# A static order of five engines laid out anew, with points of their own for each stream and for the first pair

## What is computed

```python
def reference(x, ...):
    # tok: byte embedding and six hashed n-gram embeddings, then a dense encoder
    for i, n in enumerate((3, 4, 5, 6, 7, 8)):
        idx = ngram_hash(x, n, 25000)            # float32 weighted sum mod vocab
        acc[:, :s - n + 1] += ngram_emb[i][idx] / n * sigmoid(gates[i])
    h = concat([byte_emb[x], acc / 6]) @ W_enc + b_enc
    # tower: three layers of retention (4 heads of 32, decay folded into rotary q and k) and a gelu ffn
    X = layernorm(h)
    for l in range(3):
        Y = msr(layernorm(X) * ln1_w + ln1_b, ...) + X
        X = gelu(layernorm(Y) * ln2_w + ln2_b @ ffn_w1 + ffn_b1) @ ffn_w2 + ffn_b2 + Y
    h = h + X
    # experts: each token goes to the one of 8 experts with the largest logit
    e = argmax(layernorm(h) @ Wg + bg)
    return h + relu(layernorm(h) @ W1[e] + b1[e]) @ W2[e] + b2[e]
```

## Time and profile before

| | |
|---|---|
| median of 3 runs | 2562.33 us (2554.43, 2562.33, 2565.30) |
| span of the profiled execution | 2420.6 us, 52515 instructions |
| own time of the profiled execution | not given by the page; the median lies 141.7 us above its span |
| TensorE matmul | 2230.0 us (92%) |
| VectorE | 1880.2 us (78%) |
| GpSimd | 1763.7 us (73%) |
| ScalarE | 1551.0 us (64%) |
| the chain that ended last | TensorE 74%, GpSimd 9%, VectorE 7%, issue 5% |
| TensorE's granted clock, mean | 0.979 of full |

### The profile page before, as it was taken

One profiled execution on the slowest core, in us unless ns is written; L12 is line 12 of the kernel. 1 busy time (PEld: TensorE's weight loads), 2 busy tenths in 40 slices (PEclk: granted clock), 3 DMA queues, 4 the chain that ended last, 5 costly groups with the idle time before them and its releaser, 6 DMA issues.

```text
span 2420.6 us, 52515 instructions
## 1 busy us (share of the span) xinstructions
PE 2230.0 (92%) x18308; PEld 1947.2 (80%) x18308; DVE 1880.2 (78%) x5639; ACT 1551.0 (64%) x4990; POOL 1763.7 (73%) x1764
## 2 busy tenths in 40 slices
PE   1579999999999999999999999999999999997984
PEld 0368888888888888888888888888888888886874
DVE  5757788888787888888888888787888888766543
ACT  0256677776767677777777767767677777763442
POOL 5687677777777777778777777777777774333777
PEclk9799999999999999999999999999999999997997
DMA  3552031313122222212131313121221111002875
GB/s 116 193 176 69 24 112 28 112 29 112 27 74 66 72 69 71 70 54 89 27 113 28 112 27 112 29 91 48 72 68 36 33 28 36 1 30 79 256 228 158
DMA packets 110817, 192.19 MB, mean 79 GB/s; under 512 B 24421, under 2 KB 45287, under 8 KB 110449
## 3 DMA queue, kind: packets, MB, share of 16 engines
q1 hardware_dynamic: 66928, 97.96, 11.7%
q0 software_dynamic: 33280, 67.45, 10.0%
q10 hardware_dynamic: 10368, 23.67, 3.2%
HBM read 100.30 MB, written 89.73 MB: 79 GB/s over the span
## 4 chain that ended last, share of the span: by engine, by line
PE 74%; POOL 9%; DVE 7%; issue 5%; ACT 3%; DMA 2%; ACTq 1%; POOLq 0%; SPq 0%; DVEq 0%
PE psum L1294 64%; PE psum L1315 7%; POOL grams L669 3%; PE psum L1368 3%; POOL gr L704 3%; POOL out L731 2%; DVE hid L1141 2%; ACT qm L790 1%; ACT qkT L788 1%; DMA out<-h,e_id 1%; ACT xn L801 1%; DVE side_n L1092 1%; DVE qk L1120 0%; POOL rstd L680 0%; DVE hid L1117 0%
## 5 line engine op out<-in xcount | busy, mean ns | idle before, releaser
L669 POOL DMA_INDIRECT grams<-gram_table,idx_all x768 | 779.1, 1014 | 187.7 <-issue 183.0
L1294 PE MATMUL psum<-xT,lw 128*128 128x256 f32 x1920 | 481.2, 384 | 0.1
L704 POOL TENSOR_TENSOR gr<-ms,con 128x8 f32<-128x8 f32 x192 | 319.2, 1663 | 133.1 <-DVE ms L1146 128.4
L1294 PE MATMUL psum<-lw,hid 128*128 128x129 f32 x3072 | 390.7, 276 | 3.4 <-ACT hid L820 3.4
L1294 PEld LDWEIGHTS psum<-lw,hid 128*128 128x128 f32 x3072 | 370.7, 192 | 12.9 <-issue 5.6
L680 POOL TENSOR_TENSOR rstd<-ss,con 128x2 f32<-128x2 f32 x320 | 233.5, 732 | 195.0 <-ACT squares L764 192.7
L1294 PEld LDWEIGHTS psum<-xT,lw 128*128 128x128 f32 x1920 | 340.5, 192 | 32.3 <-ACT xT L776 0.2
L820 ACT ACTIVATE hid<-psum,par 128x256 f32<-128x256 f32 x768 | 307.7, 487 | 43.2 <-PE psum L1294 40.5
L1294 PE MATMUL psum<-lw,xT 128*128 128x256 f32 (+1 forms) x1536 | 288.6, 331 | 6.5 <-ACT xT L776 6.5
L776 ACT ACTIVATE xT<-psum,par 128x256 f32<-128x256 f32 x384 | 213.9, 561 | 121.6 <-PE psum L1315 120.6
L1294 PEld LDWEIGHTS psum<-lw,xT 128*128 128x128 f32 x1536 | 250.5, 192 | 33.3 <-ACT xT L776 7.2
(11 more groups left out here) (223 smaller groups left out, 4721.2 us busy)
## 6 DMA issues: line engine op xcount, KB each, us to landing
routed_rows<-pad SPq DMA_DIRECT2D x265, 264.0 KB
grams<-expert_w ACTq DMA_DIRECT2D x45, 321.0 KB
grams<-gram_table,idx_all POOLq DMA_INDIRECT x768
grams<-routed_rows SPq DMA_DIRECT2D x80, 132.0 KB
qm<-expert_w ACTq DMA_DIRECT2D x27, 321.0 KB
xb<-x SPq DMA_DIRECT2D x32, 256.0 KB, 3.5
lw<-layer_w SPq DMA_DIRECT2D x1, 2503.5 KB, 11.8
routed_rows<-row,slot POOLq DMA_INDIRECT x128, 2.4
```

What stands on the lines that cost most here:

```text
L669: pool.indirect_dma_start(grams[s][:, g, c, :], None, gram_table, bass.IndirectOffsetOnAxis(ap=idx_all[:, g, at:at + 1], axis=0))\
L704: pool.tensor_tensor(gr[s][:, c], ms[s][:, c], const("half")[:, 0:n], ALU.pow).then_inc(y_r[s], 1)
L1294: return pe.matmul(dst, lhsT, rhs, start=start, stop=stop)
```

## The change

The program of each engine keeps its steps, its semaphores and its data; only the points change, and so the order of the steps. The table `AT` has now an entry for each of the four streams (`2 * s + h`) where it had one for each half. The first pair has a table of its own, `FIRST_AT`. The gathers of the first and second pair have a point each (`FIRST_GATHERS`, `NEXT_GATHERS`), and so have the setup steps (`SETUP_AT`). `LAGS`, `EARLY` and `CLOSING` stay. All entries of `AT` have new values; a few rows of the tables stand for all:

```diff
-LATER_GATHERS = (7.05, 12.5, 21.34, 22.17, 59.24, 65.47, 86.1, 94.55, 101.98, 104.91, 113.22, 119.36)
+LATER_GATHERS = (12.54, 16.39, 21.44, 25.43, 65.16, 67.77, 87.75, 97.67, 102.66, 105.89, 115.69, 118.65)
+SETUP_AT = {
+    "pool sums": (29.81, 32.41, -61.5, -39.17),
+    "pool rest": (43.31, 31.31),
+    "dve front": (-19.14, -58.79, -17.76, -68.98, -30.37, -90.72, -58.67, 14.16, 1.3, 22.9, 16.72),
+    "dve middle": (41.91,),
+    "dve back": (47.24, -1.87, -19.85),
+    "dve layer1": (50.64, 37.25),
+    "dve layer2": (68.28, -8.55),
+}
+FIRST_GATHERS = (
+    (-66.45, -47.46, -10.8, -68.66, -29.74, -5.51, 1.84, -28.34, -9.51, -80.01, -15.08, -63.27),
+    (-68.21, -13.83, -32.71, -15.08, -80.07, -14.35, -88.26, -32.05, -43.75, -128.7, -141.88, -3.47),
...
+NEXT_GATHERS = (
+    (27.83, -6.29, -28.85, 25.87, 37.09, -94.35, 42.14, 47.52, -1.13, 50.35, -22.49, 42.25),
...
 AT = {
-    "pe qkT": ((9.86, 8.84, 8.47), (9.32, 11.03, 9.14)),
-    "pe w1": ((5.16, 6.35, 4.1), (5.09, 6.4, 5.9)),
+    "pe qkT": ((11.26, 9.4, 9.79), (8.36, 8.33, 9.76),
+        (8.6, 9.43, 7.91), (10.56, 11.52, 9.22)),
+    "pe w1": ((4.48, 7.83, 5.35), (5.37, 3.46, 6.61),
+        (4.44, 7.87, 6.12), (4.13, 3.57, 7.24)),
...
+FIRST_AT = {
+    "dve xn1": ((10.49, -0.85, -41.79), (-4.3, 5.85, 6.58),
+        (0.74, -59.19, -0.67), (-5.43, -15.7, 3.21)),
+    "dve kv": ((-48.75, -20.26, 12.44), (14.48, 16.61, 10.66),
+        (10.58, 10.83, 0.47), (2.76, 13.62, -19.03)),
+    "dve onehot": ((-14.52,), (18.71,),
+        (33.71,), (-2.47,)),
...
-        def spaced(part, start, step):
+        def spaced(part, name):
             for n, _ in enumerate(part):
-                yield start + step * n
+                yield SETUP_AT[name][n]
...
-        def at(name, h, l=0):
-            return AT[name][h][l]
+        def at(name, it, s, h, l=0):
+            if it == 0:
+                return FIRST_AT[name][2 * s + h][l]
+            return AT[name][2 * s + h][l]
...
-                yield from spaced(mod_sum(hashes[1], REST_MOD), 31.5, 1.5)
-                yield from spaced(mod_rest(hashes[1], REST_QUOT), 39, 1)
+                yield from spaced(mod_sum(hashes[1], REST_MOD), "pool sums")
+                yield from spaced(mod_rest(hashes[1], REST_QUOT), "pool rest")
...
-                    yield (1.25 * n - 15, 30 + 2.6 * n, LATER_GATHERS[n])[min(it, 2)]
+                    yield (FIRST_GATHERS[2 * s + h], NEXT_GATHERS[2 * s + h], LATER_GATHERS)[min(it, 2)][n]
...
-                yield from spaced(hash_front(hashes[1]), 4, 3)
-                yield from spaced(hash_middle(hashes[1], 3), 38, 1)
-                yield from spaced(hash_back(hashes[1], 4), 40, 1)
-                yield from spaced(centred_layer(1), 46, 4)
-                yield from spaced(centred_layer(2), 60, 4)
+                yield from spaced(hash_front(hashes[1]), "dve front")
+                yield from spaced(hash_middle(hashes[1], 3), "dve middle")
+                yield from spaced(hash_back(hashes[1], 4), "dve back")
+                yield from spaced(centred_layer(1), "dve layer1")
+                yield from spaced(centred_layer(2), "dve layer2")
```

More of the change, by code:

```diff
@@ L1105, in attend @@
                 a, b = bank_a(s, h), bank_b(s, h)
-                yield at("dve xn1", h, l)
+                yield at("dve xn1", it, s, h, l)
                 if l == 0:
@@ L1168, in route @@
                 moments = row[s][:, :, H + 1:H + 3]
-                yield at("dve row", h)
+                yield at("dve row", it, s, h)
                 if it:
```

360 lines of the change are left out of this document (280 added, 80 removed), and 35 rows, old and new, of tables (AT, FIRST_GATHERS, NEXT_GATHERS).

## The result

| | us, median (lowest to highest) | runs |
|---|---|---|
| before | 2562.95 (2554.43 to 2565.3) | 4 |
| after | 2611.82 (2603.71 to 2612.71) | 4 |

The ratio is 1.0197 [1.0172, 1.0221]. Forecast were 2549 us and a range of 2532 to 2574.

A forecast was written before the change was run, and what follows sets the result against it. TensorE was taken to bound the kernel from about 200 us, waiting earlier while the four streams fill. Terms -8 - 1.3 - 3 - 0.5 = -12.8 us on 2562.3 gave 2549 us, range 2532 to 2574.

The forecast's parts named there:

- The base: Whole kernel: the 141.7 us between profiled span 2420.6 and median 2562.3 were taken as unchanged time around the span.
- the -8 of the first pair: First pair of batches: -8 us together, bounds -13 to +10, from gathers of pair 1 and the clock.
- The repeating order: Some 14 later pairs: -0.2 us each, -3 us in all, as the wait at scores b2 moves to qkT b2.
- third rival: Repeating pairs: w1 c1 behind qkT b2 starts 1.4 us later each pair, giving 2577 us; chance 0.12.
- the values' lead: First pair, stream a: values at 84 to 88 us in place of 96.6; keeping this lead was the -8 bound, 0 taken.
- a's projection, +6: First pair, TensorE: stream a's projection moves from 67.76 to 73 to 74 us, +6 us.
- The wait at kv a goes: First pair, TensorE: the 11.39 us wait for kv a at 91.05 vanishes, with scores a at about 81.
- gr a at 102 to 104: First pair, GpSimd: stream a gets its gr at 102 to 104 us before and after, so that part counts 0.
- Gathers of pair 1, -5: GpSimd: gathers moved into the wait before rstd2 a1 bring later steps forward, -5 us, bounds 0 and 10 gained.
- The clock, -3: First pair, TensorE: with the gaps goes part of the low clock, -3 us, bounds 0 and 3.4 gained.
- The gram sums block GpSimd: Rival, first pair: c's gram sums and stretched integer steps delay gr a by 4 us, 2553 us; chance 0.08.
- No GpSimd wait before 110: First pair, GpSimd: a sign that the forecast holds, no wait of GpSimd before 110 us.

The follow-up runs named there:

- e3: After with its tables written more compactly, the same order on every engine; 2588.86 us in its one run, in the 2526 group.
- e1: Before, unchanged, run again for a second profile; 2526.24 us, in the 2526 group.
- e14: After with accT b0 and its copy later, kv a0 back behind proj, xn1 b1 one place earlier; 2418.87 us, 0.999 of before, 2421 group.
- e16: Before's set-up, first pair and gathers of pair 1, then after's order with e14's three moves; 2574.3 us, 1.0193 of before, 2526 group.
- e11: Before with only the gathers of pair 1 at the new points; 2428.56 us, 1.0028 of before, 2421 group.
- e2: Before with the new table AT in every pair but the first and the new later gathers; 2584.83 us, 1.0239 of before, 2526 group.
- e8: Before with the gathers of all but the first two pairs replaced by a short GpSimd instruction; 2475.99 us, 0.9799 of before, 2526 group.
- e9: After with the gathers of all but the first two pairs replaced by a short GpSimd instruction; 2505.64 us, 0.9918 of before, 2526 group.
- e4: After with xn1 b1 moved ahead of z c0 on VectorE; 2649.66 us, 1.0347 of before, 2560 group.

## Why the prediction was wrong

**The base, the step that failed first.** "I take what lies around the span as unchanged": 141.7 us were ascribed to something outside the span, and nothing is there (1.8 us). They were in it: late signals and a slower experts' stage, on chips whose profile I did not have. A median that lies 6% over the profiled span was the one hint on the page, and I put it aside as a constant. It should have been a rival of its own: the profile is of another condition, and each price from it may not hold. A constant 141.7 us in both kernels would have done no harm; but the prices of the sum are from that profile too, and they did not hold. Against -12.8 us for the whole, the new order cost +23.3 us by the first scatter and +39.1 in the pairs behind it (e3 against e1). In its own condition the sum came to -2.5 us (e14, which is after with three moves), so the -8 of the first pair was wrong there too.

**The repeating order.** Forecast: -0.2 us a pair, 128.9 to 129.1, no wait at scores b2, one of 0.7 at qkT b2. In the 2421 group e14, with its three moves, has -0.22, 128.94, none, and 0.35: the mechanism was right and the new wait mis-sized by half. In the slower groups the wait at scores b2 does go too, and one at scores c1 that before has only there (0.7 us a pair each in e1). But three dependences that had enough TensorE work between them for undelayed signals have not for late ones. The waits of TensorE in ten pairs of e3:

```profile
PE psum L1398 <- ACT zp L900: 15.2, 19, 1.3
...
PE psum L1419 <- DVE xn L1157: 11.9, 10, 1.2
...
PE psum L1419 <- ACT hid L924: 7.6, 6, 1.4
```

That is 1.31 us a pair ahead of ms d2 (the first row has smaller waits too), 1.19 ahead of norm1_T b1 and 0.76 ahead of accT b0. Of the 3.06 us a pair between e1 and e3, 1.66 are more holes (5.63 against 3.97) and 1.38 are a TensorE that is busy for longer with the same instructions. The clock has a part in that: the granted clock is at half in five stretches of 3.4 us in e3's ten pairs and in ten of after's, each behind a wait of over 0.6 us and most of them behind the one at ms d2. It never is in the ten pairs of before, e1 and e14, which have 0, 2 and 0 waits over 1.0 us there (e3 27, after 25); nor is it in e16, which has 10, so a long wait alone does not do it. By these rows that is 0.9 us a pair in e3 and 1.7 in after, an estimate. "The period passes 129.16 us" was the third rival's sign, but its place, w1 c1, is not where the time went.

**The first pair.** Forecast -8, bounds -13 and +10 (the lower one leaves out the -8 of the values' lead that its own part has). In the 2421 group e14's first scatter is at 330.1 (before 329.8): +0.3, inside the bounds. Taken apart:
- *a's projection, +6.* In e14 it starts at 73.90, +6.1: right. The way there was not: xn1 a moved from 60.1 to 71.7 us, +11.6, since once behind x0 b it also waits for the rstd of b, behind b's gram sum (the 2.67 us from GpSimd in e14's row). In before the early xn1 a was of no use: ScalarE copied its transpose (xT) at 67.17 only, behind squares that started at 66.56. So 7.7 us lay between xn1 a and the projection; in e14 2.2.
- *The wait at kv a goes.* It does, in every run of after. scores a, forecast at 81, is at 80.71 in e14: right. In e3 it is at 90.5 (95.9 in e1).
- *gr a at 102 to 104.* 104.41 in e14, and 106.81 in e1, but about 115 in after (below).
- *Gathers of pair 1, -5.* Not by these gathers: alone they cost 5.5 us (e11). I had counted the gathers ahead of gr c0, gr d0 and the steps of pair 1, and not ahead of rstd2 b0, which comes first in time: 55 before, 63 in e11, 57 in after, whose other steps move too. rstd2 a1, forecast "some 5 us sooner", is at 168.4 in e14 (before 168.7), and w1 of c0 to a1 is 3 to 5 us later there in 120 to 260 us.
- *The clock, -3.* It needed the waits to go. In e14 the granted clock of 105 to 200 us is 0.87 (before 0.92), in after 0.80 (e1 0.89).

So the two terms that made up the -8, gathers and clock, are the ones that failed there.

In the slower groups the first scatter comes 23 us later than before's, 12.9 of them with pair 1 (e2). The timelines of the start of after, and two rows of e1:

```profile
51.70 1.06 DVE L1110 SCALAR_TENSOR_TENSOR hid<-win,hid 128x120 f32<-128x120 f32 x5 [5.16 <-remote]
...
58.72 0.86 DVE L1110 SCALAR_TENSOR_TENSOR hid<-win,hid 128x120 f32<-128x120 f32 x4 [5.57 <-remote]
...
82.40 0.76 DVE L1253 TENSOR_TENSOR xn<-X,rstd 128x256 f32<-128x256 f32 x2 [2.68 <-POOL rstd L893]
...
84.56 2.93 PE L1494 MATMUL psum<-lw,xT 128*128 128x256 f32 x8 [0.66 <-ACT xT L976]
...
106.84 0.96 POOL L885 TENSOR_TENSOR side_mom<-side_mom,con 128x2 f32<-128x2 f32 x1 [6.73 <-DVE side_mom L1264]
...
114.77 0.69 POOL L893 TENSOR_TENSOR rstd<-ss,con 128x2 f32<-128x2 f32 x1 [3.74 <-ACT squares L964]
...
115.43 1.90 POOL L904 TENSOR_TENSOR gr<-ms,con 128x8 f32<-128x8 f32 x1
...
119.65 1.02 POOL L869 DMA_INDIRECT grams<-gram_table,idx_all  x1 [2.32 <-DVE idx_all L1157]
```

```profile
64.96 0.86 DVE L910 SCALAR_TENSOR_TENSOR hid<-win,hid 128x120 f32<-128x120 f32 x4 [5.55 <-remote]
...
106.81 1.63 POOL L704 TENSOR_TENSOR gr<-ms,con 128x8 f32<-128x8 f32 x1
```

The hash steps that now stand ahead of x0 a are a chain on VectorE alone; two of their waits, 5.16 and 5.57 us, are for VectorE's own late signals. GpSimd issues gather after gather during the first; the last of them ends at 55.35, and the second wait at 58.72. e1 has one such wait, also ahead of its xn1 a, which is at 68.46 there and not at 60.07. Whether the gathers hold VectorE's signals back as well, no run shows. With them the projection is at 84.56, not 67.76, gr a at 115.43 and the first gather of pair 1 at 119.65. The two waits of GpSimd ahead of gr a, 6.73 and 3.74 us, are not the late signals' doing: e14 has them as well, 6.73 and 3.28 us, with gr a at 104.41 and the first gather at 108.65. They belong to the new order, in which GpSimd is ahead of VectorE's steps. "No GpSimd wait before 110" and "gr a later than 106 would be wrong": the page shows both wrong.

**The rivals.** The slower one at 2577 had the sign and 0.12 of chance, but its cause is not the one found. *The gram sums block GpSimd* (gr a 4 us late): gr a is 1.9 us late in e14, behind the two waits of GpSimd above. Its four big integer steps did not stretch: 1.40, 1.39, 1.70 and 1.70 us in e14, 1.39, 1.38, 1.70 and 1.76 before. VectorE alone paid: beside them stands also onehot, 2.97 us in e14's row at 83.05, 0.35 elsewhere.

**The kind of error.** Only 0.10 stood on slower, since both the tight spots and the costs were taken from one condition. Before lost 3.4 us a pair to the late signals (129.16 to 132.55). The new order with e14's moves lost 5.5 (128.94 in e14, 134.44 in e16), and without them it is at 135.61 (e3). My reading is that an order with no slack at many steps loses more when signals come late. It is not the only one: the new order also has more late signals (275 against 208, and 101 against 58 over 1.0 us, in the same 1300 us), and no run parts the two.

**What stays open.** What in a gather holds the signals of TensorE (e8 takes away its issue and its transfers at once, and these two were not told apart), and why chips differ; whether the experts' stage is longer by its late signals alone; what leaves e9 with 0.9 us a pair beside the scatters was read from the trace, not taken away; whether after itself would be at 2421 us in the first group; and whether an order can be found for the slower groups. All moves tried there were made by hand, one signal at a time, and one of them (e4) put its step ahead of its own input.

## What to carry to other kernels

Set the profiled execution's time against the median of the runs before any sum is made; if they differ by per cents, the profile does not show what is measured, and a chance must be kept for waits that it lacks. A hand-made order is worth its tenths of a microsecond only where every hand-over has slack for the slowest signal seen (here up to 2.7 us behind TensorE in the repeating part), above all next to indirect DMAs. Of a moved step, count the instructions ahead of every step of its queue in order of time, the first one in time above all.

## What the runs showed of the hardware

- One program takes 2421, 2526 or 2560 us by the chip. The medians of a chip used twice agree within 1 us; the single runs of one chip spread over 4 us in the first group, up to 10 in the second and up to 27 in the third, the 4944 us run left out. The clock is not the reason in the repeating part (1.00 in before, e1 and e14). In the slower groups every pair takes 3.4 us more (e1), and what stands behind the first scatter of the last pair, nearly all of it the experts' stage, 52.7 us more; in both parts signals come late.
- There, semaphore updates of TensorE come up to 2.7 us behind the end of their row in 500 to 1800 us, and all but two of after's within 2.3 us of the start of an indirect DMA on GpSimd; with no gathers (e8) none is late. VectorE's own came up to 5.6 us late, in the start alone. The profile names the longer ones "remote" in the waits, though there is one core.
- In ten places of after's ten pairs the granted clock was at half for 3.4 us (0.50 in 550.00 to 553.40), each behind a wait of TensorE of over 0.6 us; in before's, whose longest wait is 0.75, and in e16's, with waits up to 1.2, it was nowhere.
- A step can be dearer by its neighbour: onehot on VectorE took 2.97 us beside GpSimd's integer steps, 0.35 us elsewhere, and the integer steps themselves took no longer (1.40 against 1.39 us).
